# A gated cross-attention and mixture-of-experts kernel on one core: fixed first blocks, attention on raw x, two tokens a partition

## The reference, cut to what matters

```python
def _L0_xattn_ref(teacher_logits, teacher_features, Wq, bq, Wk, bk):
    query = jnp.einsum('bnc,dc->bnd', teacher_features, Wq) + bq
    key = jnp.einsum('bnc,dc->bnd', teacher_features, Wk) + bk
    attention = jax.nn.softmax(jnp.einsum('bnd,bmd->bnm', query, key), axis=-1)
    return jnp.einsum('bln,bmn->blm', teacher_logits, attention)
def _L0_ffn_ref(x, rw1, rw2, w1, b1, w2, b2):
    probs = jax.nn.softmax(_gelu(x @ rw1) @ rw2, axis=-1)
    wgt, idx = jax.lax.top_k(probs, TOP_K)              # 2 of 8
    out = jnp.zeros_like(x)
    for e in range(E):
        Ye = _gelu(x @ w1[e] + b1[e]) @ w2[e] + b2[e]   # 256 -> 1024 -> 256
        Ce = _gelu(b1[e]) @ w2[e] + b2[e]
        for k in range(TOP_K):
            mask = idx[..., k] == e
            active = jnp.any(mask).astype(x.dtype)
            out = out + active * wgt[..., k:k + 1] * jnp.where(mask[..., None], Ye, Ce)
    return out
x = x + jnp.tanh(g_xattn[0]) * _L0_xattn_ref(_layernorm(x), ctx_1024, Wq, bq, Wk, bk)
x = x + jnp.tanh(g_ffn[0]) * _L0_ffn_ref(_layernorm(x), rw1, rw2, w1, b1, w2, b2)
```

## Time and profile before

| | us |
|---|---|
| median of 3 runs (233.81 to 234.52) | 233.97 |
| the profiled execution, its own time | 233.93 |
| its span, first to last instruction | 232.1 |
| mean granted TensorE clock over the span, share of full | 0.865 |
| busy: TensorE matmul / VectorE / GpSimd / ScalarE | 173.3 / 156.6 / 113.5 / 96.1 |

### The profile page before, as it was taken

How to read it: one execution, slowest core, us unless ns; L and a number is a source line. 1 busy time by engine, 2 the same in 40 slices (tenths; PEclk the granted TensorE clock), 3 DMA queues, 4 the chain that set the end, 5 groups by cost and what they waited for, 6 DMA issues and landing times.

```text
span 232.1 us, 5641 instructions
## 1 busy us (share of the span) xinstructions
PE 173.3 (75%) x1708; PEld 142.1 (61%) x1709; DVE 156.6 (67%) x315; ACT 96.1 (41%) x230; POOL 113.5 (49%) x144
## 2 busy tenths in 40 slices
PE   7875549935920029724999999999999999999690
PEld 2454437514810014514988899999999999987360
DVE  1399998799999989977573555555555555554265
ACT  1459524952956750340333343333334444432000
POOL 0033373795559903999035655555555555322200
PEclk9999775996875555895899999999999999999955
DMA  6994554679398830419115566566666666650196
GB/s 179 292 385 146 181 181 116 208 236 309 140 329 280 252 124 3 136 52 358 47 55 220 200 235 246 230 245 246 236 238 245 246 241 237 218 203 25 46 291 229
DMA packets 25809, 46.93 MB, mean 202 GB/s; under 512 B 2917, under 2 KB 17983, under 8 KB 25794
## 3 DMA queue, kind: packets, MB, share of 16 engines
q1 hardware_dynamic: 21952, 40.82, 49.7%
q0 software_dynamic: 1872, 4.73, 6.6%
q10 hardware_dynamic: 1970, 1.19, 1.8%
HBM read 23.64 MB, written 4.60 MB: 122 GB/s over the span
## 4 chain that ended last, share of the span: by engine, by line
PE 45%; DVE 36%; DMA 7%; issue 5%; ACT 3%; SPq 1%; DVEq 1%; ACTq 0%; POOL 0%; POOLq 0%
PE bank L1082 7%; PE bank L1072 7%; PE bank L1074 7%; PE bank L1073 7%; PE bank L1084 7%; PE bank L1083 7%; DVE lnx L584 4%; DVE w_lo L561 4%; DMA xs<-in_x 4%; DVE cf L787 3%; DMA stage<-y_table 2%; ACT w_hi L421 2%; DVE cf L701 2%; PE bank L956 2%; DVE E L703 2%
## 5 line engine op out<-in xcount | busy, mean ns | idle before, releaser
L534 ACT ACTIVATE lnx<-bank,b1T 128x128 f32<-128x128 f32 x152 | 43.2, 368 | 69.1 <-PE bank L1074 64.9
L336 POOL TENSOR_TENSOR w_lo<-stage,w_hi 128x1024 bf16<-128x1024 f32 x23 | 50.4, 2215 | 36.2 <-ACT w_hi L421 36.2
L1072 PE MATMUL bank<-cfT,stage 128*128 128x128 f16 x272 | 52.6, 219 | 0.0
L1073 PE MATMUL bank<-cfT,stage 128*128 128x128 bf16 x272 | 52.6, 219 | 0.0
L1074 PE MATMUL bank<-cfT,stage 128*128 128x128 f16 x272 | 52.6, 219 | 0.0
L1082 PE MATMUL bank<-w_hi,cf 128*128 (+1 forms) x152 | 42.0, 276 | 6.2 <-DVE lnT L789 6.1
L787 DVE CAST cf<-lnx 128x512 f16<-128x512 f32 x38 | 22.3, 586 | 33.9 <-issue 22.1
L1083 PE MATMUL bank<-w_lo,cf 128*128 (+1 forms) x152 | 41.9, 276 | 0.0
L1084 PE MATMUL bank<-w_hi,lnT 128*128 (+1 forms) x152 | 41.9, 276 | 0.0
L421 ACT ACTIVATE w_hi<-stage 128x1024 f16<-128x1024 f32 x32 | 32.4, 1052 | 20.0 <-DMA stage<-in_L_ffn_w 17.6
L342 POOL TENSOR_TENSOR held<-cst 128x1 f32<-128x1 f32 x39 | 10.2, 262 | 41.7 <-DVE qT L796 40.0
(11 more groups left out here) (165 smaller groups left out, 285.7 us busy)
## 6 DMA issues: line engine op xcount, KB each, us to landing
stage<-in_L_ffn_w SPq DMA_DIRECT2D x32, 512.0 KB, 4.3
stage<-w_hi SPq DMA_DIRECT2D x18, 512.0 KB
stage<-w_lo SPq DMA_DIRECT2D x18, 512.0 KB
stage<-y_table SPq DMA_DIRECT2D x8, 256.0 KB, 4.9
xs<-in_x SPq DMA_DIRECT2D x1, 1024.0 KB, 8.2
out<-stage SPq DMA_DIRECT2D x4, 256.0 KB, 2.9
cf<-in_ctx SPq DMA_DIRECT2D x1, 512.0 KB, 4.9
x_table<-cfT ACTq DMA_DIRECT2D x2, 256.0 KB, 3.6
```

The source lines that it names most:

```text
L336: nc.gpsimd.tensor_tensor(out=w_lo[:, q, :], in0=stage[:, q % RING, :], in1=w_hi[:, q, :], op=ALU.subtract).then_inc(lo_pool, 1)
L534: last = nc.scalar.activation(hidden[u][:, cc * P:cc * P + P], bank[(0 if u == 0 else 6) + half][:, c * P:c * P + P], ACT.Gelu, bias=b1T[: ...
L1072: mm(o, wh, xh[:, d, :], start=(d == 0), stop=False)
L1073: mm(o, wh, xl[:, d, :], start=False, stop=False)
```

## The change: what it does

1. **Places.** The first 128 slots of expert e are block e, always; only what an expert has above 128 gets further blocks from block 8 on. Blocks 0 to 7 (`NS = N_EXP`) are written out with the expert as a constant; they read w1 in place and wait only for the quarters they need. The ranks are counted twice in two PSUM banks, the second time with the expert's number added. `fetch_w1` begins at block 8.
2. **Conversions.** `DVE_QUARTERS` and all positions change: ScalarE has 16 quarters done before the choice's exponential instead of 28, 4 right after, 12 between the gelus of blocks 0 to 4. GpSimd has 13 quarters behind it when the gathers begin (less its VectorE ones), the others lie between gathers and scatters of blocks 0 to 7. GpSimd's subtraction of a quarter becomes 4 instructions of 256 columns.
3. **Attention on raw x.** `lnT_tr` transposes x itself. The row's 1/deviation is multiplied in at the residual (`pull`), its mean becomes a constant per token (`shift`) that the second norm does not see and that a 17th row of ones in `cb` brings back at the end. The first `normalise` goes. Exponentials stay in PSUM and are scaled from there. The second norm is done batch by batch. The copies of identities and constants move ahead of the attention. The 24 filler matmuls before the router (L900) go.
4. **Token split.** The high part moves to ScalarE (`token_high`), the rest to GpSimd (`token_low`).
5. **Two tokens a partition.** x, context, output, `x_table` and `y_table` are read and written as "(p j)" instead of "(j p)", so a partition's two rows lie side by side in HBM: pieces of 2 KB instead of 1 KB for x, results and output, 1 KB instead of 512 bytes for the context. x comes as two DMAs.
6. **End.** The row loads of `cb` are issued before the last scatters are waited for.
7. Static blocks use the index column in place: no L346 or L354 and, for gathers, no `hold`.

```diff
+PIECE = 256
+CAT = 2 * N_EXP + 1
-        DVE_QUARTERS = (3, 7, 11, 15, 18, 25, 27, 28, 30)
-        LATE = 25
+        DVE_QUARTERS = (7, 13, 14, 15, 16, 17, 18, 22, 25, 28, 31)
...
 # SyncE
-            sp.dma_start(xs[:, :, :], x.rearrange("b (j p) n -> p (b j) n", p=P)).then_inc(in_x, 16)
+            for h in range(2):
+                sp.dma_start(xs[:, 4 * h:4 * h + 4, :],
+                             x[2 * h:2 * h + 2, :, :].rearrange("b (p j) n -> p b j n", p=P)).then_inc(in_x[h], 16)
...
+            for u in range(2):
+                sp.wait_ge(scattered[u], 16 * JS)
+            sp.dma_start(cb[0:N_EXP, :], y_table[ZERO_TOKEN:ZERO_TOKEN + N_EXP, :]).then_inc(in_cb, 16)
             sp.wait_ge(scattered[0], 16 * jl + 16)
             sp.wait_ge(scattered[1], 16 * odd)
-            sp.dma_start(cb[0:N_EXP, :], y_table[ZERO_TOKEN:ZERO_TOKEN + N_EXP, :]).then_inc(in_cb, 16)
...
 # GpSimd
-            lows(0, LATE)
+            lows(0, 5)
+            token_low(0)
+            token_low(1)
+            lows(5, 7)
+            token_low(2)
+            token_low(3)
+            lows(7, 13)
...
+            for i in range(4):
+                gather(i, i % 2)
+            lows(13, 21)
+            refill(4, 0, 0, 16)
+            refill(5, 1, 1, 16)
+            lows(21, 24)
+            refill(6, 0, 2, 16)
+            wait(index_ready, 2)
+            lows(24, 27)
+            put(0, 0)
+            refill(7, 1, 3, 16)
+            lows(27, 28)
+            put(1, 1)
+            refill(NS, 0, 4, 32)
+            lows(28, 30)
+            put(2, 0)
+            refill(NS + 1, 1, 5, 32)
+            lows(30, QUARTERS)
+            put(3, 1)
+            put(4, 0)
+            put(5, 1)
...
 # ScalarE, after the exponentials
+            router_gelu(2)
+            send(0)
+            router_gelu(3)
+            token_high(2)
+            token_high(3)
+            send(1)
+            high(7, 10)
+            send(2)
+            high(10, 11)
+            send(3)
+            high(11, 16)
             act.wait_ge(dlg_ready, 1)
             nc.scalar.activation(elg[:, :, :], dlg[:, :, :], ACT.Exp).then_inc(elg_ready, 1)
-            high(28, QUARTERS)
             nc.scalar.activation(warm[:, :], tg[:, 0:1], ACT.Gelu)
+            high(16, 20)
...
+            after = {(0, 0): (20, 21), (0, 1): (21, 22), (1, 0): (22, 23), (1, 1): (23, 24), (2, 0): (24, 25),
+                     (2, 1): (25, 27), (3, 0): (27, 28), (3, 1): (28, 30), (4, 0): (30, 31), (4, 1): (31, 32)}
...
 # VectorE, attention and second norm
+            step(nc.vector.tensor_scalar(pull[:, :], rstd[:, :], tg[:, 0:1], None, ALU.mult))
+                for t in (2 * b, 2 * b + 1):
+                    nc.vector.scalar_tensor_tensor(out=xs[:, t, :], in0=bank[3 + b][:, L * (t % 2):L * (t % 2) + L],
+                                                   scalar=pull[:, t:t + 1], in1=xs[:, t, :],
+                                                   op0=ALU.mult, op1=ALU.add).then_inc(x2_ready, 1)
...
+            second_norm(2)
+            residual(3)
+            second_stats(3)
+            second_norm(3)
             low(7)
...
 # VectorE, after yidx
-            low(25)
-            low(27)
-            low(28)
+            low(13)
+            low(14)
+            low(15)
+            xT_copy(0, 0)
+            low(16)
+            xT_copy(1, 1)
+            low(17)
+            hidden_split(0, 0, 0)
+            between = {0: (18,), 1: (22,), 2: (25,), 3: (28,), 5: (31,)}
+            for i in range(NS - 1):
+                u = i % 2
+                xT_copy(i + 2, u)
+                hidden_split(i, u, 1)
+                hidden_split(i + 1, 1 - u, 0)
+                for q in between.get(i, ()):
+                    low(q)
...
+                y_copy(i, u)
...
 # TensorE
-            keep_busy(24, 1, w_hi[:, 0, 0:512])
...
+            ranks(2, True)
+            ranks(3, False)
...
+            for i in range(NS):
+                u = i % 2
+                tokens_tr(i + 1, 1 - u)
+                wait_weights(pe, QPE * i + 1)
+                for c in range(HC):
+                    up(i, u, i, c)
+                    if i:
+                        down(i - 1, 1 - u, i - 1, c)
```

759 lines of the change are left out of this document (389 added, 370 removed).

## The result

The changed kernel takes **226.92 us** (median of 4 runs, 224.95 to 227.73) against 233.89 of the kernel before on the same chip: ratio 0.970, 95% interval 0.962 to 0.978. Faster, as forecast, but by 7.0 us where 19.7 were forecast, and outside the range of 205 to 225. The profiled execution has a span of 225.8 us and an own time of 227.73, 13.4 over the forecast.

| us | before | forecast | after | miss |
|---|---|---|---|---|
| choice starts | 68.3 | 57.5 | 63.5 | +6.0 |
| choice | 12.5 | 4.9 | 4.5 | -0.4 |
| slots and indices | 9.7 | 11.9 | 12.0 | +0.1 |
| indices to first product | 5.7 | 5.0 | 6.7 | +1.7 |
| products | 118.0 | 116.2 | 121.3 | +5.1 |

What follows compares the result with a forecast made beforehand. VectorE was taken to bound everything up to the token indices, TensorE the products from 132.7 us. Six steps, summed along the timeline, brought the span from 232.1 to 212.5 us; with 1.83 outside it, 214.3, range 205 to 225.

Steps and rivals of the forecast that it cites:

- Step 1: Attention and router up to the choice: the choice starts at 57.5 us, 68.3 before, bounds 50 and 66.
- Rival B: Attention bound by round trips between TensorE, ScalarE and VectorE at the lower clock: choice starts at 66, 222.8 us; chance 0.18.
- Step 2: The choice: 4.9 us, 12.7 before, as small GpSimd pieces no longer block VectorE's six operations for long.
- Step 3: Slots and indices: 11.9 us, 9.6 before, with 3 us more for one-hots meeting GpSimd's pieces.
- Step 4: From the indices to the first product: 5.0 us, 5.7 before; first product at 79.3.
- Step 5: The products: 116.2 us, 118.0 before, from 106.7 without stall plus 9.5 of stalls.
- 5 us of room: In the products: last quarter converted by 118, due by block 8 at 123; the first w1 fetch must fit too.
- rival C: In the products: GpSimd's queue holds the static blocks through late scatters, 7 us more, 221 us; chance 0.12.
- Rival D: VectorE starves beside GpSimd's short pieces in choice, slots and products: 21 us more, 235.5 us, slower; chance 0.06.
- Step 6: The end: 17.0 us, 17.8 before, 0.4 from early `cb` loads and 0.4 from 2 KB pieces.
- Rival A: Batches overlap in the attention and pieces cost nothing in choice and slots: 205 us; chance 0.20.
- E: Rival: static blocks still wait for nearly all quarters, so time won in front is lost: 231 to 234 us; chance 0.02.

Runs made afterwards that it cites:

- x3: Changed kernel with 28 filler matmuls put between the steps of attention and router; 219.6 us, ratio 0.939 to the kernel before.
- y4: Kernel before the change with eighteen more filler matmuls between the mixes of its attention; 231.7 us, ratio 0.989.
- x6: Changed kernel with ScalarE's conversion of quarter 7 moved ahead of the router's last gelu; 226.2 us, ratio 0.952.
- x1: Changed kernel with GpSimd's low parts in whole quarters of 1024 columns again, not pieces of 256; 229.8 us, ratio 0.985.
- x4: Changed kernel with TensorE transposing block 1's tokens behind block 0's first products, not ahead of them; 227.5 us, ratio 0.971.
- w1: Changed kernel with x3's fillers and the edits of z1 (quarters to VectorE), x2, y1 and x6 together; 213.2 us, ratio 0.911.
- x7: Changed kernel with VectorE making the low part of quarter 31 one block earlier, behind block 4's splits; 224.8 us, ratio 0.964.
- y1: Changed kernel with x3's fillers, and SyncE's wait before fetching w1 set at quarter 29 in place of 31; 221.1 us.
- x5: Changed kernel with nearly all of GpSimd's low parts from quarter 19 on left out, those parts zero; 219.5 us, ratio 0.940.
- y2: Changed kernel with x3's fillers, and GpSimd waiting for each piece to be complete before starting the next; 228.2 us, ratio 0.972.
- x2: Changed kernel with the scatters of blocks 0 to 3 each one group of low parts earlier on GpSimd's queue; 226.5 us, ratio 0.968.
- x8: Changed kernel reading each token's results in 1 KB pieces, as before the change, in place of 2 KB; 225.1 us, ratio 0.965.
- z4: Changed kernel with x3's fillers and the edits of x2, y1, x6 and x4 together; 217.3 us, ratio 0.923.
- y3: y2 (fillers, and a gap after each GpSimd piece) with the edits of y1, x7 and x4 added; 224.7 us, ratio 0.957.
- z3: z2 with GpSimd waiting for the completion of each piece from quarter 14 on; 220.3 us, ratio 0.944.
- z1: Changed kernel with x3's fillers, and VectorE making the low parts of quarters 20, 23 and 26 in place of GpSimd; 216.9 us, ratio 0.930.
- z2: Changed kernel with x3's fillers and the edits of x2 (earlier scatters) and y1 (earlier w1 fetch); 218.1 us, ratio 0.934.
- w2: Changed kernel with VectorE making quarters 20, 23 and 26 in place of GpSimd, without fillers; 225.9 us, ratio 0.965.

## Why the prediction was right or wrong

**Step 1, the choice starts at 57.5: wrong by 6.0 us, the largest miss.** In the terms of the sum, read from the changed kernel's timeline:

| us | forecast | after | x3 |
|---|---|---|---|
| VectorE's first statistics of x start | 10 | 12.2 | 11.9 |
| its work up to its last normalisation | 25 | 24.5 | 25.4 |
| its waits up to there | 11 | 14.4 | 9.3 |
| from there to the last logits | 8 | 9.7 | 6.8 |
| from there to the choice | 3.5 | 2.8 | 3.2 |

The step that failed is the costing of the waits and of the router. Both came from rows at the full clock, the round trip of 3.5 from a mix of 1.96 us (41.03) and the 4.0 of a router batch, and the sum let the filler matmuls go "at no cost". At 0.50 a mix alone is 1.8 us longer. x3, at 0.98, has 5.1 us less of waits and 2.8 less of router, and its choice starts 6.9 us earlier. Rival B named this mechanism, with the choice at 66. The error was to argue from a bound that the change itself removes: in the kernel before, VectorE set the pace and a slower TensorE cost little (y4: 2.4 us); in the changed one nothing covers it.

What is not shown is that the 24 removed fillers would have kept the clock up. They stood behind the last mix (42.84 to 48.18 in the kernel before), and the changed kernel's mixes are at 0.50 from 24 us on, ahead of that place. The kernel before, with them, had slow mixes too: its batches 1 and 2 took 2.83 and 3.75 us. No run puts these 24 back alone, so their part in the router's 1.7 us is open.

By the rule of the Trainium skill (TensorE: Matmul & The Clock Gate, Part 1), the array's clock is halved after little work. The trace agrees: the 0.50 from 24 us on follows four microseconds in which TensorE was busy for 0.9.

The first row of the table is a miss that fillers do not touch. TensorE's first matmul on data starts at 9.19 us, before at 7.08. It waits for the small loads of the attention's biases, the last of which lands 6.8 us after its issue, before 4.7. x is now loaded ahead of other things and was the reason to forecast 10; that the new order of loads delays the biases fits, and no run tried it. The last row was in the sum and right in kind (x6). That x3 nearly meets 57.5 is in part luck: it starts late and waits less than the sum had.

**Step 2, the choice, 4.9: right** (4.5), and for its reason: x1 brings the six long operations back. Nothing in it lost more than about half a microsecond, where the prediction had a piece of 0.53.

**Step 3, slots, 11.9: right** (12.0). x1's 9.1, with whole quarters and GpSimd idle in that stage, bears out that about 3 us are GpSimd's pieces beside VectorE's operations; the one-hots' mean rose from 305 to 444 ns. The prediction did not see that these 3 us are the price of the small pieces.

**Step 4, 5.0: wrong by 1.7**, the second gather, overlooked, since block 1's transposes stand ahead of block 0's `up`. x4 gives the 5.0 exactly; its time did not fall, so this miss cost the whole nothing that can be seen.

**Step 5, products 116.2: wrong by 5.1.** The step that failed is the base of 106.7, in which TensorE works at the full clock throughout. The sum added stalls to it as idle time only, 9.5 us, and TensorE was idle for 9.5 us; but it was busy for 111.8, since it does not work at the full clock at their start (0.62 in the first 3 us) and behind the long stalls, and that is the whole 5.1. In w1, at 1.00, it was busy for 107.3. That the idle time came out equal is luck in part: 2.2 us of it is a wait ahead of block 8, for which the sum had nothing, and in the first 45 us of the products TensorE was idle for 6.5 us and not 9.

Mis-sized was also the quarter on GpSimd: 2.1 to 2.7 in the sum, 3.2 measured in the products. The "5 us of room" went: the last quarter, forecast 39 us after the first product, was there after 46, and block 8's w1 was fetched late. But an earlier fetch alone gave the products nothing (x7, y1). This is rival C, a queue of GpSimd that holds the static blocks; it asked for 7 us, x5 gives back 6.6, and w1, with the fillers and four more edits, 6.2. Through which of its effects (scatters late, runs of pieces that block VectorE, quarters late) the queue costs most is open: y2 shows the first, the 4.28 us cast the second, and neither x2 nor y1 shortened the products by its own edit.

The prediction called the step wrong if ScalarE's `high` waits long for DMA. It did wait, 4.85 us up to 85.86, ahead of the first product, and 1.1 us in all inside the products. w1 has the same wait (4.30 us up to 78.68) and the fewest us of products but x5, so this wait does not set them.

Rival D's mark, a VectorE instruction over 2 us beside a run of pieces, was there (4.28), but once; it cost TensorE 2.9 us, not 21. By the rule of the Trainium skill (SBUF — State Buffer, SBUF: two separate sides), the loser is blocked until the other's instruction ends; the trace disagrees, as it did before the change, since that cast was held until the last of eight instructions had ended. What chooses between half a piece and eight of them stays open.

**Step 6, 17.0: wrong by 0.8 in this profile**; the 17.0 lies inside the 16.3 to 17.4 us of the other runs with 2 KB pieces. The early `cb` is real, but VectorE's wait for the first results was 4.97 us, before 4.65, and 2 KB pieces show no saving (x8).

Rival A fell: batches did not overlap. E fell: the static blocks start with their own quarters. The forecast's chances had B and C as alternatives, at 0.18 and 0.12, with 222.8 and 221. They are independent, and both came, in part; the case of both, about 230, was not in the range.

## What to carry to other kernels

When a change takes away the work that bounds a stage, cost again everything that was hidden under it, TensorE's clock first: put filler matmuls into its waits and look at the clock before judging the change. A stall of TensorE has two prices, its idle time and the slower matmuls behind it; a sum needs both. An edit that makes a helper engine's instructions smaller is paid for in its total time; add that to its queue and read what stands behind it (here scatters, then a buffer, then TensorE). Rivals with separate mechanisms add up, so the range has to hold their sum.

## What was not expected of the hardware

GpSimd's pieces in a row can hold VectorE for all their length, but seldom: of some 140 VectorE instructions in the products of x6 one, a low part (1.22 us undisturbed), took 6.36. Timelines of VectorE and GpSimd, x6:

```profile
94.61 6.36 DVE L627 TENSOR_TENSOR w_lo<-stage,w_hi 128x1024 bf16<-128x1024 f32 x1
```

```profile
94.81 5.06 POOL L358 TENSOR_TENSOR w_lo<-stage,w_hi 128x256 bf16<-128x256 f32 x8
```

The eight pieces lie wholly inside it, at 0.63 us each, the pace that GpSimd has while VectorE is idle (four in 2.55 us at 54.07 in the changed kernel): VectorE got nothing at all. VectorE's instruction even began 0.2 us before the first piece.

The same low part, of quarter 18, took 6.49 us in x8 and 6.45 in z4, again beginning 0.3 us before a run of eight pieces. All three profiles with such a block are of the longest execution of their kernel (x6 220.6 to 230.0 us, x8 224.6 to 228.6, z4 214.0 to 219.1), and no profile of another execution has one. That fits the block making the spread; it is not shown, since only the profiled execution shows one.

With a completed piece before the next (y2, y3, z3) no VectorE instruction took over 2.1 us, at 0.4 us more a quarter (the shortest takes 2.90 us in y2, 2.54 in z2). But x4, x5, z1, z2, w1 and w2 have none either without such gaps, so these three do not show that gaps prevent it.
